# A two-layer graph network: layer 0 in steps of two groups, with eight edge slots

## The reference

```python
def layer0(x, src, dst, e32):              # W1 is 128x128, W2 is 128x48
    tmp = concatenate([x[dst], x[src], e32], axis=1)    # 48 + 48 + 32 = 128
    h   = relu(tmp @ W1 + b1)
    return segment_sum(h @ W2 + b2, dst)
def layer1(x, src, dst, e48):
    return (1 + eps) * x + segment_sum(relu(x[src] + e48), dst)
x = layernorm(x + layer0(x, src, dst, edge_attr_32))
x = layernorm(x + layer1(x, src, dst, edge_attr_48))
```

## Time and profile before

| | |
|---|---|
| median of 3 runs | 4393.23 us |
| profiled execution | 4396.01 us |
| its span | 4394.2 us |
| mean granted TensorE clock | 0.849 |
| PE busy | 3762.4 us, 86% |
| POOL busy | 2898.7 us, 66% |
| DVE busy | 1853.6 us, 42% |
| ACT busy | 744.0 us, 17% |

### The profile page before, as it was taken

One profiled execution on the slowest core, in us unless ns is written; L12 is line 12 of the kernel. 1 busy time (PEld: TensorE's weight loads), 2 busy tenths in 40 slices (PEclk: granted clock), 3 DMA queues, 4 the chain that ended last, 5 costly groups with the idle time before them and its releaser, 6 DMA issues.

```text
span 4394.2 us, 54802 instructions
## 1 busy us (share of the span) xinstructions
PE 3762.4 (86%) x20440; PEld 2846.8 (65%) x20440; DVE 1853.6 (42%) x3723; ACT 744.0 (17%) x1666; POOL 2898.7 (66%) x2756
## 2 busy tenths in 40 slices
PE   5788888888888888888888889888889888898897
PEld 3566666556666665655666677667677767676776
DVE  1222222222222222221223667566566666665665
ACT  1222222222222222222221000000000000000111
POOL 6666666666666666665664677667667677767674
PEclk9688888988888888876667889889889999898887
DMA  4122222222222122211221222222222222222221
GB/s 98 30 33 31 31 34 31 31 31 32 32 32 33 31 33 32 31 29 33 33 33 33 45 46 51 43 45 47 43 45 49 45 46 47 47 48 46 47 52 41
DMA packets 401844, 176.02 MB, mean 40 GB/s; under 512 B 279724, under 2 KB 400738, under 8 KB 401474
## 3 DMA queue, kind: packets, MB, share of 16 engines
q0 software_dynamic: 88064, 67.81, 10.9%
q1 hardware_dynamic: 311458, 104.16, 10.4%
q10 hardware_dynamic: 2050, 0.48, 0.1%
HBM read 167.21 MB, written 5.00 MB: 39 GB/s over the span
## 4 chain that ended last, share of the span: by engine, by line
PE 52%; another core or an unknown queue 19%; issue 12%; POOL 7%; DVE 7%; ACT 2%; DMA 1%; SPq 0%; DVEq 0%; POOLq 0%
PE ps_h L783 10%; PE ps_t L783 9%; PE ps_m L706 8%; POOL edge L507 7%; PE ps_h L756 7%; PE ps_sums L697 6%; PE ps_nodes L728 5%; PE ps_t L743 3%; PE ps_nodes L793 2%; PE ps_a L746 2%; DVE picked L997 1%; DVE at_place L988 1%; DVE at_place L943 1%; DVE msg L925 1%
## 5 line engine op out<-in xcount | busy, mean ns | idle before, releaser
L507 POOL DMA_INDIRECT edge<-x,resid_sb x1494 | 1491.9, 999 | 857.6 <-issue 440.6
L507 POOL DMA_INDIRECT edge<-x_dram,resid_sb x1258 | 1406.5, 1118 | 614.8 <-issue 374.7
L921 DVE TENSOR_TENSOR acc<-acc,ps_sums 48x48 f32 x782 | 154.6, 198 | 1833.2 <-remote 1010.9
L783 PE MATMUL ps_h<-x_parts,at_place 125*128 125x480 f32 x3080 | 778.2, 405 | 48.7 <-issue 41.8
L783 PE MATMUL ps_t<-x_parts,at_place 125*128 125x480 f32 x3040 | 780.0, 410 | 44.8 <-issue 42.2
L783 PEld LDWEIGHTS ps_h<-x_parts,at_place 125*128 125x128 f32 x3080 | 611.0, 201 | 179.8 <-issue 74.9
L783 PEld LDWEIGHTS ps_t<-x_parts,at_place 125*128 125x128 f32 x3040 | 606.6, 203 | 175.0 <-issue 76.0
L697 PE MATMUL ps_sums<-edge,msg 128*48 128x48 f32 x6256 | 441.5, 222 | 269.2 <-issue 147.0
L697 PEld LDWEIGHTS ps_sums<-edge,msg 128*48 128x48 f32 x6256 | 345.8, 132 | 440.2 <-issue 288.5
L706 PE MATMUL ps_m<-w_sb,hT 128*128 128x48 f32 x3128 | 516.5, 317 | 40.9 <-ACT hT L614 39.4
L756 PE MATMUL ps_h<-edgeT,w_edge 128*128 128x512 f32 x782 | 550.1, 793 | 0.0
(11 more groups left out here) (66 smaller groups left out, 1842.4 us busy)
## 6 DMA issues: line engine op xcount, KB each, us to landing
e_sb<-e SPq DMA_DIRECT2D x196, 192.0 KB
edge<-e SPq DMA_DIRECT2D x196, 128.0 KB
edge<-x,resid_sb POOLq DMA_INDIRECT x1494
place_row<-rows_dram SPq DMA_DIRECT2D x376, 62.5 KB
edge<-x_dram,resid_sb POOLq DMA_INDIRECT x1258
x_win<-xT SPq DMA_DIRECT2D x391, 9.0 KB
acc<-xT SPq DMA_DIRECT2D x10, 234.4 KB
feats<-x SPq DMA_DIRECT2D x10, 234.4 KB
```

What stands on the lines that cost most here:

```text
L507: pool.indirect_dma_start(out=cols, out_offset=None, in_=rows_of, in_offset=bass.IndirectOffsetOnAxis(ap=index, axis=0)).then_inc(done, 16)
L783: last = nc.tensor.matmul(ps_picked[q % BANKS], lhsT=at_place[:, q % PLACED, c, :], rhs=x1_parts[:, c, part, :], start=(c == 0 and part == ...
```

## The change

Layer 0 goes through pairs of groups: 196 pair steps and three more. In pair step p TensorE transposes both groups of p, does one product for both groups' window columns, the sums of pair p-3, the outputs of p-2, the pre-activations of p-1, and then the products of a pick. `edge` has 8 slots, in both layers; `ps_a` and `ps_s` share a bank, one group in its lower and one in its upper half; `ps_m` and `edgeT` are held for more groups. VectorE copies the window products to `w_edge`, not ScalarE. Picks follow a table, `plan_pairs`: three in four steps (20, 20, 10 and 10 matmuls), 126 in all, into a bank of their own. So 1438 gathers remain in layer 0. Layer 1's table is as before. To make room, `dst_t`, `spread`, `staged` and others share memory with buffers that are free at the time. x1 chunks are stored three iterations later, the last three at the end of the layer.

```diff
+def plan_pairs(first, last):
+    picks, units = [], {}
+    for s in range(first, last - 2, 4):
+        for begin, end in ((s, s), (s + 1, s + 1), (s + 2, s + 3)):
+            q, each = len(picks), CHUNKS // (end - begin + 1)
+            for step in range(begin, end + 1):
+                units[step] = [(q, (step - begin) * each + c) for c in range(each)]
+            picks.append((2 * (end + 2) + 1, begin - 1, end + 1))
+    return picks, units
...
-        edge = sb("edge", [P, UNROLL, TILES, P])
+        edge = sb("edge", [P, RING, TILES, P])
...
# GpSimd
-                    wait_group(pool, S[read], i, u, back=UNROLL)
+                    wait_for(pool, S[read], g - RING)
...
# ScalarE, layer 0
+                for g in pair(p):
+                    wait_for(act, S0["trans"], g)
+                    nc.scalar.activation(edgeT[:, g % UNROLL, :], ps_t[g % 2][:, :], ACT.Copy).then_inc(S0["edgeT"], 1)
...
+                for g in pair(p - 1):
+                    wait_for(act, S0["pre"], g)
+                    nc.scalar.activation(hT[:, g % 2, :], ps_h[g % 2][:, :], ACT.Relu, bias=b1_sb[:, :]).then_inc(S0["h"], 1)
...
# TensorE, layer 0
+                if pair(p):
...
+                    wait_for(pe, S0["edgeT"], 2 * p - 1)
+                    for g in pair(p):
+                        transposes(g)
+                    wait_for(pe, *((S0["stat"], 2 * p - 1) if p < 4 else (S0["acc"], 2 * p - 7)))
+                    first = 2 * p % UNROLL
+                    nc.tensor.matmul(ps_as[:, 0:H], lhsT=x_win[:, first:first + 2, :].rearrange("d g n -> d (g n)"), rhs=w1_dst[:, :],
+                                     start=True, stop=True).then_inc(S0["awin"], 1)
...
+                for g in pair(p - 3):
+                    sum_messages(S0, g)
+                for g in pair(p - 2):
+                    output_layer(g)
...
+                products = PRODUCTS0.get(p, ())
+                pick_rows(S0, products[:-1], [ps_early])
+                if products:
+                    wait_for(pe, S0["onehot"], pair(p + 1)[-1])
+                pick_rows(S0, products[-1:], [ps_early])
...
# VectorE, layer 0
+                if pair(p - 3):
+                    wait_for(dve, S0["seg"], pair(p - 3)[-1])
+                if pair(p):
+                    place_windows(p)
+                for g in pair(p - 3):
+                    accumulate(S0, g)
...
+                for g in pair(p + 1):
+                    onehots(S0, g, iota_sb[:, :])
...
+                offset_messages(p - 2)
+                for q, (_, find, _) in enumerate(PLAN0):
+                    if find == p:
+                        find_places(S0, q)
```

More of the change, by code:

```diff
@@ L716, in turn_places @@
                 last.then_inc(s_turned, 1)
-            def pick_early(j, chunks):
-                for c in chunks:
-                    if c == 0:
-                        if j == FIRST_PICK:
-                            pe.wait_ge(S0["parts"], PARTS * PIECES)
-                        else:
-                            pe.wait_ge(S0["picked"], 2 * early_to(j - 1) - 1)
-                        pe.wait_ge(S0["places"], early_to(j))
-                    for part in range(PARTS):
-                        last = nc.tensor.matmul(ps_early, lhsT=at_place[:, 0, c, :], rhs=x1_parts[:, c, part, :],
-                                                start=(c == 0 and part == 0), stop=(c == CHUNKS - 1 and part == PARTS - 1))
-                    if c == CHUNKS - 1:
-                        last.then_inc(S0["ten"], 1)
@@ new lines, in transposes, with edges_there @@
+            def transposes(g):
+                pe.wait_ge(S0["rows"][g % RING], landed(S0, g))
+                for t in range(TILES):
+                    if t == 1:
+                        pe.wait_ge(S0["window"][g % UNROLL], 16 * (g // UNROLL) + 16)
+                    last = nc.tensor.transpose(ps_t[g % 2][:, t * P:(t + 1) * P], edge[:, g % RING, t, :], ident_sb[:, :])
+                last.then_inc(S0["trans"], 1)
+            def edges_there(p):
+                pe.wait_ge(S0["edges"][p % (RING // 2)], 16 * (p // (RING // 2)) + 16)
@@ new lines, in find_places, with select_rows @@
+            def find_places(S, q):
+                dve.wait_ge(S["row"][q % PLACED], 16 * turns(q))
+                nc.vector.tensor_tensor(at_place[:, q % PLACED, :, :], place_row[:, q % PLACED, :].unsqueeze(1).to_broadcast([NP, CHUNKS, P]),
+                                        places_sb[:, :].unsqueeze(2).to_broadcast([NP, CHUNKS, P]), ALU.is_equal).then_inc(S["places"], 1)
+            def select_rows(S, picks, q, banks):
+                group = picks[q][0]
+                if q > 0:
+                    dve.wait_ge(S["picked"], 2 * q)
+                dve.wait_ge(S["ten"], q + 1)
```

417 lines of the change are left out of this document (206 added, 211 removed).

## The result

| | before | after |
|---|---|---|
| median beside each other (17 runs each) | 4402.06 us | 4437.45 us (4387.19 to 4462.73) |
| ratio | | 1.0058, 95% interval 1.003 to 1.0086 |
| span of the profiled execution | 4394.2 us | 4413.9 us |
| mean granted clock | 0.849 | 0.863 |
| first to last gather of layer 0 | 2345.1 us | 2324.3 us |

The kernel became slower by 0.6%. Two later comparisons gave 1.0106 (1.0066 to 1.0146) and 1.0098 (1.0075 to 1.0122). In these two executions layer 0, where nearly all of the change lies, ends as late as before, and layer 1, where only the ring differs, is longer. Over all traces that were taken with either code (three and four), layer 1's first gather starts at 2383 us in the mean before and at 2400 us after, 17 us later.

What follows compares the result with a forecast made beforehand. GpSimd was taken to set the pace through gathers and waits for `edge` slots, with TensorE near the bound. From 4396 us, less 215 in layer 0 and 20 in layer 1, plus 5, less 2.8: 4163 us; range 3960 to 4430 us.

Steps and rivals of the forecast that it cites:

- the third rival: Both layers: twice the slots lengthen the blocks of late TensorE results; about 4570 us, or 4420 with a fifth of that; 14%.
- Eight slots: `edge` ring, both layers: GpSimd runs up to eight groups ahead, taking away at most all 403 us of waits, at least none.
- The rate of TensorE: Layer 0: between 0.86 (2030 us) and 0.79 (2210 us) of full speed, middle 2130 us; forecast wrong below 0.76.
- TensorE's work of 1746 us at full clock: Layer 0 after the change: 1568 us, plus 244 for added products, less 66 for shared column products.
- GpSimd's 1906 us: Layer 0, GpSimd alone: 1942 us less 73 for 56 fewer gathers, plus up to 37 for gathers beside comparisons.
- The price of a pick: Layer 0: each added comparison on VectorE lengthens a gather from 0.94 to 1.60 us, up to 56 x 0.66 = 37 us.
- VectorE places the columns: Layer 0: window copies move from ScalarE to VectorE at 0.26 us each; cost 0, bounds 0 and 100 us.
- Products: Layer 0, TensorE: 1120 more products at 0.218 us, 244 us more at full clock.
- one product for two groups' columns: Layer 0, TensorE: 196 window products instead of 391, 0.34 us each, 66 us less.
- Layer 1: Only the ring changes there: 20 us gained, bounds 90 us gained and, by the third rival, 185 us lost.
- The seam: Gap before layer 1's first gather: may grow 0 to 15 us, taken as 5, as three x1 chunks are stored, not two.
- Rival one: GpSimd alone bounds layer 0, TensorE staying near 2.4 GHz: layer 0 1920 to 1990 us, whole 3880 to 4020 us; 12%.

## Why the prediction was wrong

The forecast was 4163 us, faster, and the time is 4437. It comes out on the side of the third rival, "the longer ring makes the late releases longer; slower", which had 14%; the range of 3960 to 4430 us ended just below it.

**The step that failed** is *Eight slots*: "It is the part that can take the 403 us away". I took GpSimd's waits as waits that alternate with TensorE's and that a longer ring absorbs. The ring was in fact full (3.6 of 4 groups), and a full ring says that what empties it is slower in the mean. The text had the other bound in the same breath, "returns nothing when TensorE is slower in the mean", and the count of the lead would have told which: in the kernel before, GpSimd was already as far ahead as it may be. The waits went from 381 to 463 us in the same window.

**The rate of TensorE** failed with it. I chose the middle between 0.86 and 0.79 of full speed; measured is 1746 / 2324 = 0.75, below the 0.76 that I had named as the point where the forecast is wrong. Before it was 1568 / 2345 = 0.67. A rate was the wrong form for this loss, and the kernel before says so: by the same two rates its 1568 us would take 1823 or 1985 us, and they took 2345. TensorE isn't slowed in proportion: what it loses is the blocks, which are there only with a dense stream of gathers. 439 us less work gave 95 us, and taking the stream away gave 1772 us with all the work in it. The third rival's sum for layer 0, 2331 us at the rate of 1000 to 1500, is what happened (2324, 2343 and 2332 us in three traces).

**What held.** TensorE's work of 1746 us at full clock: with one gather a group layer 0 took 1753 and 1772 us, at a clock of 0.97 over the whole of it, or 1700 and 1719 us at full clock. GpSimd's 1906 us is near: layer 0 took 1905 us in the run without late releases and most products, and with all of them the gathers need 1923 to 1929 us (the durations and 0.30 us each), in the changed kernel's own traces 1876 to 1884.

**The price of a pick** was too low. 0.66 us came from one gather of 1.60 us, and that is less than the usual. In the kernel before, 85 gathers overlap its 70 comparisons. They take 1.82 us in the mean, up to 2.60, and have 74 us of excess, 1.06 us a pick. The earlier trace rows had it too: 1494 x 0.999 less 1494 x 0.944 is 82 us, 1.17 us a pick. The Trainium skill (SBUF — State Buffer, Who interferes with whom) has a tensor_tensor not stalling the DMAs that GpSimd issues, with a reason that it marks as inferred, but contending with GpSimd's reads when both its inputs lie in SBUF. The trace disagrees with the first a second time (1.92 us at 1012.96). It would agree with the second: the comparison and the one-hots have both inputs in SBUF, and the selection, which takes one from PSUM, lengthens nothing (0.944 us). No run tests what a gather reads.

*VectorE places the columns*: two copies take 0.61 us, 0.29 each in the mean, where I took 0.26. No loss from them is seen, but inside a block they wait 14.46 us like all else. *Products* and *one product for two groups' columns* cost what they were priced at, and did not matter.

**Layer 1** was the 20 us that I had as a gain and is 20 us of loss: from its first gather to the end 2028.9, 2041.9 and 2015.4 us, mean 2029, against 2006.5 and 2011.8 before. The rival had the longer blocks and put their price at 185 us, with the blocks half as long again. They did grow by half (9.1 to 13.9 us), but there were a third fewer of them. The cost that the traces show is that more groups are left when the last gather is done, 36 us of work where it was 12. I had reckoned that the number stays while the length grows.

**The seam** was priced at 5 us. From the end of layer 0's last sums to layer 1's first gather it is 2384.98 - 2373.06 = 11.9 us, and before 2387.68 - 2375.58 = 12.1 us: nothing. The longer gap in GpSimd's row is its longer lead.

Rival one (GpSimd alone, 12%) is how layer 0 looks in the sessions without late releases, where GpSimd hardly waits. Even there it isn't known to bring a gain: the changed kernel itself was not timed in one. Its versions with fewer picks or a shorter lead lose 0.4 to 1.3% there.

## What to carry to other kernels

Before pricing a longer ring, count how full the present one is. Where the producer is nearly always at its limit (3.6 of 4 groups here), the consumer is the slower one in the mean. More slots then didn't take the waits away (381 to 463 us here) and left more work behind the last load.

Before a rate from another stretch is used to forecast, put the kernel as it is through the same formula; 1985 us for a measured 2345 would have stopped this one. A loss that comes in blocks isn't a rate. Look at what the other engines do when a block ends, and take that away once: here one gather a group brought TensorE's 1746 us from 0.75 to 0.99 of full speed.

Work that replaces a gather has to be priced with what it does to all gathers that remain, not to one: 1.16 us of lengthening for 1.24 us saved.

## What the hardware showed that was not expected

The same program takes 3802 to 3807 us in some sessions and 4397 to 4413 us in others, and two chips each showed both. In the latter TensorE's releases come late in blocks; in the former all of them come within 0.02 us. Everything else in the rows agrees (a lone gather 0.94 us, the next 0.30 us later, `at_place` 1.48 us). What differs between the sessions isn't known, and nothing in a kernel selected it.

Blocks were seen only with a dense stream of gathers (1.25 us apart), and the long ones end some 2 us after it stops. How GpSimd's gathers hold up TensorE's semaphore events was not found. Code loading was looked at: the packets of the instruction queue come every 17 to 35 us in layer 0, 24 us in the mean, and blocks begin in all parts of that interval, two in three in its first half. With one gather a group TensorE runs the same instructions and there are no blocks, so code loading alone doesn't make them; whether it starts them stays open.

A comparison on VectorE (1.48 us, both inputs in SBUF) lengthens the gathers that it overlaps from 0.94 to as much as 2.60 us; a selection, with one input in PSUM, lengthens none.
